# A vision tower's tile loop on one core: the head's step written in another order on five engines

## The reference

```
xs = concat(x, x shifted right, left, down, up)           # 5 x 3 channels
y  = conv16x16(xs) + conv_b ;  y = layernorm(y)*gamma+beta ;  h = y @ dense_w + dense_b
h  = h + silu(n @ wg + bg) * (q k^T * decay) v            # n = layernorm(h), 8 heads, 16 tokens of an image
m  = layernorm(h);  scores = sigmoid(m @ gate_w.T);  two best of 64 experts
h  = h + silu(m @ sw1)*(m @ sw3) @ sw2 + sum of the two experts' (silu(m w1)*(m w3)) w2, weighted
```

## Time and profile before

| | us |
|---|---|
| median of 3 runs (lowest to highest) | 272.69 (272.01 to 273.07) |
| the profiled execution's own time | 270.12 |
| its span in the profile | 268.3 |
| PE matmul busy | 183.7 (68%) |
| DVE busy | 129.0 (48%) |
| POOL busy | 120.0 (45%) |
| ACT busy | 86.6 (32%) |
| mean granted TensorE clock | 0.814 of full speed |

### The profile page before, as it was taken

The page is one execution under the profiler, slowest core; times in us unless marked ns, Lnnn a source line. Parts: engine busy times, 40 slices in busy tenths (PEclk is TensorE's granted clock), DMA queues, the critical chain, the costliest instruction groups (busy, mean ns, idle before and its releaser), DMA issues.

```text
span 268.3 us, 4422 instructions
## 1 busy us (share of the span) xinstructions
PE 183.7 (68%) x1385; PEld 128.3 (48%) x1385; DVE 129.0 (48%) x446; ACT 86.6 (32%) x228; POOL 120.0 (45%) x208
## 2 busy tenths in 40 slices
PE   0985688988888877987898531499999975552000
PEld 0432354655555545755566420399989953331000
DVE  2523154257776665457555627244645542223811
ACT  0030654344545564443554110145444411110000
POOL 3055222045655566455366675013232007777770
PEclk9999999579999997557555555599999999999555
DMA  7999999834665552244000001778843261222541
GB/s 268 372 374 374 416 400 429 319 145 176 174 175 168 162 127 76 49 88 100 10 22 20 22 20 38 194 191 245 275 145 113 68 170 43 51 59 53 147 98 29
DMA packets 29213, 42.95 MB, mean 160 GB/s; under 512 B 2752, under 2 KB 21376, under 8 KB 27904
## 3 DMA queue, kind: packets, MB, share of 16 engines
q1 hardware_dynamic: 26176, 35.27, 39.9%
q0 software_dynamic: 3008, 7.34, 9.4%
HBM read 24.45 MB, written 18.15 MB: 159 GB/s over the span
## 4 chain that ended last, share of the span: by engine, by line
PE 43%; POOL 24%; issue 13%; DMA 8%; DVE 5%; ACT 4%; SPq 2%; POOLq 1%; DVEq 0%
POOL X L1060 11%; PE bank L571 6%; POOL RS L1009 6%; PE scores L467 4%; DMA C<-cst 4%; PE bank L580 4%; PE bank L413 4%; PE bank L453 3%; PE scores L580 3%; ACT xrow L662 3%; PE bank L497 3%; PE bank L445 2%; POOL NM L1012 2%; PE bank L563 2%; PE bank L438 2%
## 5 line engine op out<-in xcount | busy, mean ns | idle before, releaser
L1033 POOL DMA_INDIRECT expert_rows<-xrow,slots x32 | 32.5, 1015 | 31.4 <-issue 30.3
L1060 POOL DMA_INDIRECT X<-expert_rows,slots x32 | 30.5, 955 | 23.0 <-DMA expert_rows<-ys 13.5
L413 PE MATMUL bank<-X,W 128*128 128x512 f32 x48 | 27.5, 684 | 7.4 <-DVE W L758 6.8
L673 ACT ACTIVATE qm<-bank,bqm,C 128x128 f32<-128x128 f32 x64 | 24.1, 456 | 10.0 <-PE bank L446 10.0
L922 DVE TENSOR_TENSOR hT<-bank,gs 64x512 f32<-64x512 f32 x17 | 11.8, 694 | 24.5 <-ACT gs L727 24.5
L1048 POOL DMA_DIRECT2D expert_rows<-ys x12 | 9.1, 760 | 32.2 <-DVE ys L935 32.2
L478 PE MATMUL scores<-vg,ST 64*64 64x16 f32 x512 | 21.8, 226 | 0.3 <-DVE ST L853 0.3
L478 PEld LDWEIGHTS scores<-vg,ST 64*64 64x64 f32 x512 | 20.2, 162 | 3.7 <-issue 2.6
L785 DVE BATCH_NORM_STATS2 stats<-bank 128x6 f32<-128x128 f32 x16 | 4.8, 299 | 33.6 <-PE bank L424 33.6
L435 PE MATMUL bank<-C,xrow 128*128 128x128 f32 x16 | 5.8, 366 | 20.3 <-ACT xrow L662 20.3
L662 ACT ACTIVATE xrow<-h,NM,RS 128x128 f32<-128x128 f32 x16 | 7.9, 493 | 36.3 <-POOL NM L1012 36.3
(11 more groups left out here) (131 smaller groups left out, 382.6 us busy)
## 6 DMA issues: line engine op xcount, KB each, us to landing
expert_rows<-EW SPq DMA_DIRECT2D x10, 1024.0 KB, 19.4
X<-xp SPq DMA_DIRECT2D x12, 512.0 KB, 14.1
xb<-expert_rows SPq DMA_DIRECT2D x16, 256.0 KB, 3.9
expert_rows<-ys POOLq DMA_DIRECT2D x12, 256.0 KB, 3.2
EW<-w SPq DMA_DIRECT2D x4, 512.0 KB, 5.4
EW<-wp SPq DMA_DIRECT2D x3, 640.0 KB, 6.2
XE<-xe SPq DMA_DIRECT2D x4, 384.0 KB, 15.7
expert_rows<-ys SPq DMA_DIRECT2D x4, 256.0 KB, 2.5
```

Of the source, the lines that this page charges most:

```text
L413: mm = nc.tensor.matmul(CONV[:, :], w, x, start=(j == 0), stop=(j == NCH + 1))
L673: nc.scalar.activation(qm[:, t % 2, m], QK[:, 0:P], ACT.Identity, bias=bqm[:, m:m + 1], scale=head[:, m:m + 1])
L1033: pool.indirect_dma_start(buf, bass.IndirectOffsetOnAxis(ap=slots[:, k, t:t + 1], axis=0), xrow[:, t % XR], None).then_inc(sent[t % XR], 16)
L1060: pool.indirect_dma_start(pr[:, t, k], None, buf, bass.IndirectOffsetOnAxis(ap=slots[:, k, t:t + 1], axis=0)).then_inc(pr_in[t // TS], 16)
```

## The change

Nothing is computed differently: the same instructions are issued, in another order on PE, DVE, POOL and ACT. (One register or branch row of POOL's list differs.) SP is not touched.

- PE: `conv_step(i, 0)` comes ahead of `attend(i-3)`. `embed(i+1)` moves from the end of the step to just behind `attend`. `scores(i-2)` comes ahead of `turn(i)`. `conv_step(i, 1)` stands between `turn(i)` and `logits(i-4)`.
- DVE: `decay_scores` opens the step and works for tile i-3 (it was last in the step, for tile i-2); `choose` and `embedded` follow; `attended` is cut in two, `gated` (the product that frees the attention's bank) and `attended` (add and statistics), and `y_stats(i+1)` stands between them. `y_stats(0)` is done ahead of the loop.
- POOL: the two sends of a tile are issued one step later (`send(i-6, k)`), and those of the last tile after the loop.
- ACT: `evac_y` comes ahead of `evac_qk` in the steps that have it.

```diff
             embed(0)
             for i in range(LAST):
+                conv_step(i, 0)
                 if 0 <= i - 3 < NT:
                     attend(i - 3)
-                conv_step(i, 0)
+                if i + 1 < NT:
+                    embed(i + 1)
                 if 0 <= i - 5 < NT:
                     places(i - 5)
+                if 0 <= i - 2 < NT:
+                    scores(i - 2)
                 if FIRST2 <= i <= LAST2:
                     turn(i)
-                if 0 <= i - 2 < NT:
-                    scores(i - 2)
+                conv_step(i, 1)
                 if 0 <= i - 4 < NT:
                     logits(i - 4)
                 if 0 <= i - 1 < NT:
                     project(i - 1)
-                conv_step(i, 1)
-                if i + 1 < NT:
-                    embed(i + 1)
...
+                if i % TG == 2 and i // TG + 1 < NG:
+                    evac_y(i // TG + 1)
                 if 0 <= i - 1 < NT:
                     evac_qk(i - 1)
                     evac_vg(i - 1)
-                if i % TG == 2 and i // TG + 1 < NG:
-                    evac_y(i // TG + 1)
...
+            y_stats(0)
             for i in range(LAST):
-                if i < NT:
-                    y_stats(i)
+                if 0 <= i - 3 < NT:
+                    decay_scores(i - 3)
                 if 0 <= i - 5 < NT:
                     choose(i - 5)
+                if i < NT:
+                    embedded(i)
+                if 0 <= i - 3 < NT:
+                    gated(i - 3)
+                if i + 1 < NT:
+                    y_stats(i + 1)
                 if 0 <= i - 3 < NT:
                     attended(i - 3)
                 if 0 <= i - 5 < NT:
                     place(i - 5)
-                if i < NT:
-                    embedded(i)
-                if 0 <= i - 2 < NT:
-                    decay_scores(i - 2)
...
                 if 0 <= i - 5 < NT:
                     accumulate(i - 5)
+                if 0 <= i - 6 < NT:
                     for k in range(TOPK):
-                        send(i - 5, k)
+                        send(i - 6, k)
+            for k in range(TOPK):
+                send(NT - 1, k)
```

More of the change, by code:

```diff
@@ L801, in choose, with gated @@
                                         ALU.is_equal).then_inc(oh_ready, 1)
-            def attended(t):
+            def gated(t):
                 dve.wait_ge(av_ps, t + 1)
@@ L810, in attended @@
                 ins.then_inc(av_read, 1)
+            def attended(t):
                 dve.wait_ge(av_read, t + 1)
```

## The result

The changed kernel takes 241.41 us, the median of 4 runs (239.66 to 244.80); the kernel before, measured beside it, takes 272.88 us (272.01 to 275.69). The ratio is 0.881 with a 95% interval of 0.869 to 0.893: 31.5 us faster, where 25.7 were forecast. The medians take in all runs and the ratio only the fast ones, so it is not the quotient of the two medians. The profiled execution of the changed kernel took 244.8 us, with a span of 243.0 us; it was the slowest of its four runs.

A forecast was written before the change was run, and what follows sets the result against it. A once-a-step ring of waits through `turn` and `embed` bound the head; afterwards the queues would. 4.4 + 11.2 + 12.5 + 0 - 2.4 = 25.7 us off 270.12 gives 244.4; carried to the median 272.69, 247.0 us, range 241 to 260.

The forecast's parts named there:

- the drain: Head's steps 16 to 18: left at 20.16 us for half clock, gain 0, 3.6 us at best.
- steps 4 to 10: Head steps with convolution chunks: 53.79 us to 42.6, seven steps of 6.08, a gain of 11.2 us.
- steps 11 to 15: Head steps without convolution: 40.10 us to 27.6 at full clock, five steps of 5.51, a gain of 12.5 us.
- the end: From the last `RS` to the last send's end: 9.5 us to 11.9, a loss of 2.4 us.
- steps 1 to 3: Early head steps: 6.36 us each to 4.9, a gain of 4.4 us, with bounds 0 and 8.
- `embed` ahead of `turn` opens the ring: Head steps: the long ring of waits, 7.1 us once a step, closes over two steps, allowing about 5 us each.
- PE's floor: Steps with chunks at full clock: 7.10 us less 1.02 of waiting leaves PE's own queue 6.08 us, the highest floor.
- POOL's floor of 5.51: POOL's work per step, read from a drain step where it hardly waits; bounds steps from 11 on.
- At half clock the gain nearly vanishes: Steps 11 to 15 at half clock take 7.7 us each, 38.5 in all, leaving a gain of 1.6 us.
- rival 1: Clock at half from step 11 on: gain there 1.6 us instead of 12.5, kernel 257.9 us; chance 0.27.
- Rival 3: Hand-overs between engines add up: steps of 7.0 us with and without chunks, kernel 260.8 us; chance 0.08.
- Rival 4: Clock falls to half in the steps with chunks: 10.3 us each, kernel slower at 287.5 us; chance 0.05.

The follow-up runs named there:

- again: The changed kernel unaltered, run again in the first job: 273.37 us, median of 6 runs from 257.53 to 282.77; the kernel before took 285.47 there.
- again3: The changed kernel unaltered, run again in the third job: 244.20 us, ratio 0.899 to the kernel before; its profiled execution took 240.19 us.
- no_lag: The changed kernel with each tile's sends back behind its own accumulate, not one step later: 287.01 us, ratio 1.007 to the kernel before.
- lag_only: The kernel before with only the sends issued one step later: 283.15 us, against 285.47 for the kernel before.
- again2: The changed kernel unaltered, run again in the second job: 248.85 us, 4 runs from 243.32 to 250.92.
- chunk_last: The changed kernel with conv_step(i, 1) moved back to the step's end: 289.55 us, ratio 1.017 to the kernel before.
- a_keep_b: The changed kernel plus unread 128x512 matmuls, one per step 11 to 19, one more from step 16; third job: 240.15 us, ratio 0.882 to before.
- a_keep: Same kernel as a_keep_b, the changed one plus unread matmuls in steps 11 to 19, in the second job: 240.26 us, ratio 0.882 to before.
- a_keep_early: The a_keep_b kernel plus seven more unread matmuls in steps 0 to 3: 241.77 us, ratio 0.886 to the kernel before.
- b_keep: The kernel before plus two unread matmuls in each step from 11 on, where the chunks stood: 271.81 us, ratio 0.989 to the kernel before.

## Why the prediction was wrong, and where it was right

**The step that failed is the last line of the sum:** "The median of the three runs is 2.6 us above that execution, so I carry the difference over". Before, the profiled execution was faster than all the others; with the change it was the slowest of four, 3.4 us above the median. Where an execution lies among its runs goes with the stretches in which its clock is at half (`again` to `again3`), and that differs from execution to execution. Nothing of it could be carried over. The range was shifted with it: from 241 it misses 240.2, which is the ratio of 0.881 applied to the 272.69 shown, and without the shift it begins at 238.4.

**Four terms of the sum were too long as well, the drain most of all.** The forecast lies 6.8 us above 240.2, and the carried 2.6 are the smaller part. In `again3`, an execution of 240.19 us, steps 4 to 10 are 0.9 us shorter than forecast, steps 11 to 15 0.8, the end 0.9, and the drain, whose gain was put at nothing, 1.6. Together that is the other 4.2.

**That the sum gave 244.4 and the first profiled execution took 244.8 is in part luck.** The same four terms are about 4 us too long there too, but that execution lost 2.7 us to the half clock in steps 1 to 3, began step 1 0.8 us later and had a second part 0.9 us longer.

Point by point:

- **`embed` ahead of `turn` opens the ring.** Right by the chains: the wait for `xrow` is gone, `RS` isn't in the chain of a chunk step, and distances fell from 7.10 to between 5.33 and 6.25, but for the step of the first send. `no_lag` and `lag_only` show that order and lag are both needed; no run moves `embed` alone, so its share of the new order against DVE's is argued and not shown.
- **"PE's floor" of 6.08.** Mis-sized. Subtracting one named wait from a step of before doesn't leave PE's own work. The ring of PE and `gated` takes 5.79, and three steps run at POOL's 5.33. The term came out near, 41.5 against 42.6, because the step of the first send takes 7.87 (54.26 to 62.13), which I had put at 6.08. POOL sits idle for 2.72 us ahead of that send. What it waits for stays open: the last of the eight zero fills that the program makes it wait for is issued at 26.8 us, and none takes longer than 25.0 us to land. The stall was there before too (2.92 us), and I counted it away, so that the term came out by luck.
- **Steps 1 to 3.** 14.7 was right where the clock held (14.54 in `again3`) and 2.7 us short where it fell twice.
- **POOL's floor of 5.51.** 5.33, mis-sized: the row of the drain had a little waiting in it. DVE's floor of 5.10 was not in the prediction, though the earlier trace rows showed DVE busy for 27.14 of 40.95 us: at 5.3 us a step that had to come close.
- **"At half clock the gain nearly vanishes".** Right in kind and priced too low: 8.1 to 9.2 us a step instead of 7.7. In the profile of `again` rival 1 did happen. In the profile of the result it did not: the clock fell at about 110 us, as forecast.
- **The lag.** Right that it takes the wait for `slots` off POOL. I took it for a gain of its own. `no_lag` and `lag_only` show that it is worth about 1% alone (283.15 against 285.47 us, too scattered for a ratio), and that without it the order is worth nothing.
- **The drain.** Left as it was, 20.2, for no row; 18.8 and 18.5 measured at half clock, 16.1 with the clock held. The lag alone took it to 18.04 in `lag_only`, for the reason that the prediction itself gives: POOL no longer waits for `slots`.
- **The end.** 11.9 against 11.04: a pair of sends was priced at 2.97 from a row with 0.61 us of idle time in it, and the last four stand 1.3 us apart, 2.5 a pair.
- **Rival 3**, steps of 7.0 us from hand-overs, did not come. The ring that it names is not in the chain of these steps; one that the prediction does not list is, through ACT's projections and `gated`, 5.33 us in steps 13 to 15.
- **Rival 4**, the clock falling in chunk steps, did not come in the profile of the result. `again` and `again2` have it for about 4 us each, `chunk_last` for longer.

The clock: from 107 to 109 us PE was busy for 0.89 of 2.00 us (windows of the changed kernel), and the clock fell behind it, at about 110 us. The Trainium skill, in "TensorE: Matmul & The Clock Gate", section "What's actually happening", ties the fall to an idle stretch. This trace agrees only in part, as the earlier trace rows did: PE was less busy there but not idle, and it then stayed at half with 12.87 of 17.00 us busy. Nor do show the swings that rival 1 reads in them: they show a fall and two long stretches at half. With one or two more wide matmuls in each step the clock stayed at 1.00 from 82 to 130 us in `a_keep_b` and to 126 in `a_keep`. It was not whole in the other two: 0.75 from 122 to 126 us in `a_keep_early`, 0.57 from 106 to 110 in `b_keep`.

## What to carry to other kernels

When queues that are served in order form a ring, moving one instruction only pays once no other instruction closes the same ring: write the ring down for each engine's order before and after, and test each part alone and left out, because here neither the order nor the lag gained more than about 1% by itself and together they gave 12%. Take a floor from a step in which that engine really never waits, and list the floors of all the engines, not just the highest two. Compare a sum with the execution it was made against, never shift it by the distance to a median; and where a stretch leaves TensorE partly busy, price both clocks, and consider a few unread wide matmuls there.

## What the runs showed of the hardware

- The same kernel on the same chip lies anywhere between 243.3 and 250.9 us (four runs), in the order of its mean clock; matmuls that nobody reads gave 238.7 to 244.0 beside it, with the median 8.6 us lower. In the third job the medians were 4.1 us apart. In the kernel before the same matmuls were worth 1%, and its runs still lay 11.8 us apart.
- Two nearly equal quiet stretches (PE busy 0.30 and 0.31 of 2.00 us, from 22 to 24 us) led to a fall in one execution and to none in the other.
- Two indirect sends back to back cost POOL 2.3 us from the start of the first to the end of the second, and 2.8 with the 0.44 us ahead of them, over half of its 5.33 us step.
- One job had an end of 20.6 us instead of 7.5 behind the last gather, in all four kernels profiled, and waits of up to 18.5 us whose releaser the traces don't have. What made it so stays open.
